# Graph-transformer layer: preparation of the edge loop by groups of x, and the rows of its first four steps gathered ahead

## What is computed

```python
xn = _layernorm(x, axis=-1)
...
x_l = (x @ W_l.T + b_l).reshape(n, HEADS, DIMS)
x_r = (x @ W_r.T + b_r).reshape(n, HEADS, DIMS)
...
s = x_l[src] + x_r[dst] + e_feat
s = jax.nn.leaky_relu(s, NEG_SLOPE)
alpha = jnp.einsum('ehc,hc->eh', s, att)
...
out = jax.ops.segment_sum(alpha[..., None] * x_l[src], dst, num_segments=n)
return out.reshape(n, FEAT) + bias
```

## Time and profile before

| | us |
|---|---|
| median of three runs | 3488.56 (3485.78 to 3489.42) |
| the profiled execution | 3486.59 |
| its span, first to last instruction | 3484.9 |
| preparation, to the edge loop's first instruction | 138.59 |
| edge loop's steps | from there to about 1410 |
| rest: own part, mixer, experts | about 1410 to the end |

### The profile page before, as it was taken

The page is one execution under the profiler, slowest core; times in us unless marked ns, Lnnn a source line. Parts: engine busy times, 40 slices in busy tenths (PEclk is TensorE's granted clock), DMA queues, the critical chain, the costliest instruction groups (busy, mean ns, idle before and its releaser), DMA issues. The chain is left out here.

```text
span 3484.9 us, 52064 instructions
## 1 busy us (share of the span) xinstructions
PE 3136.0 (90%) x14323; PEld 2542.8 (73%) x14324; DVE 1877.1 (54%) x3779; ACT 1357.1 (39%) x4647; POOL 1244.5 (36%) x1197
## 2 busy tenths in 40 slices
PE   2799999999999999557998899889989986999988
PEld 1577777777777777346777677767767775888877
DVE  5577877777777877865436343643454340111002
ACT  0047767767777766431223122222312211222232
POOL 2276666666666664113103010300020016000016
PEclk9899999999999999678999999999989978999999
DMA  5576776677676676251101011000000043333333
GB/s 135 155 190 167 168 167 167 164 165 166 166 166 164 166 167 131 78 183 30 30 14 34 23 34 36 8 1 14 27 37 1 1 128 104 113 123 123 115 113 107
DMA packets 301651, 355.64 MB, mean 102 GB/s; under 512 B 164806, under 2 KB 223771, under 8 KB 297545
## 3 DMA queue, kind: packets, MB, share of 16 engines
q0 software_dynamic: 67472, 178.15, 20.1%
q1 hardware_dynamic: 233510, 173.64, 18.8%
q10 hardware_dynamic: 560, 2.35, 0.2%
HBM read 298.03 MB, written 54.91 MB: 101 GB/s over the span
## 5 line engine op out<-in xcount | busy, mean ns | idle before, releaser
L1311 PE MATMUL a_pS<-g_xr,a_lt 128*128 x1680 | 522.2, 393 | 28.0 <-DMA XS<-xl_d,a_ix 22.9
L1294 POOL DMA_INDIRECT a_g<-xl_d,a_ix x480 | 461.4, 961 | 222.4 <-PE a_pS L1312 135.0
L1405 ACT ACTIVATE b_m<-a_g,c_pcx 128x64 f32<-128x64 f32 x1856 | 454.6, 333 | 0.0
L1319 PE MATMUL b_pM<-b_m,b_oh 128*112 128x281 f32 x1680 | 445.3, 404 | 5.3 <-DVE g_acc L1447 3.5
L1440 DVE SCALAR_TENSOR_TENSOR a_r<-a_pS,g_attx 128x528 f32<-128x528 f32 x420 | 296.6, 706 | 243.8 <-PE a_pS L1312 234.8
L1294 POOL DMA_INDIRECT XS<-xl_d,a_ix x360 | 345.2, 959 | 135.3 <-issue 91.5
L113 POOL TENSOR_TENSOR m_rstd<-m_ve,m_mhalf 125x5 f32<-125x5 f32 x45 | 53.1, 1180 | 928.4 <-DVE m_ve L103 919.9
L1311 PEld LDWEIGHTS a_pS<-g_xr,a_lt 128*128 128x128 f32 x1680 | 310.0, 191 | 90.2 <-issue 33.3
L1319 PEld LDWEIGHTS b_pM<-b_m,b_oh 128*112 128x112 f32 x1680 | 292.1, 177 | 102.1 <-issue 11.4
L421 PE MATMUL m_pH<-m_h,m_w 128*128 128x312 f32 (+1 forms) x1280 | 341.9, 428 | 7.7 <-DVE m_h L566 7.7
L1405 ACT ACTIVATE b_m<-XS,c_pcx 128x64 f32<-128x64 f32 x1424 | 348.5, 333 | 0.0
(11 more groups left out here) (371 smaller groups left out, 4410.0 us busy)
## 6 DMA issues: line engine op xcount, KB each, us to landing
a_db<-dl_d SPq DMA_DIRECT2D x212, 224.0 KB
f_w<-in_ffn_W1p SPq DMA_DIRECT2D x32, 1024.0 KB
m_w<-in_mix_W SPq DMA_DIRECT2D x8, 1024.0 KB
f_w<-in_ffn_W2p SPq DMA_DIRECT2D x8, 1024.0 KB
a_g<-xl_d,a_ix POOLq DMA_INDIRECT x480, 5.7
xg_d<-m_zero POOLq DMA_DIRECT2D x1, 7168.0 KB, 30.5
a_lt<-eat_d SPq DMA_DIRECT2D x214, 32.0 KB, 4.1
eat_d<-a_stage SPq DMA_DIRECT2D x15, 448.0 KB
```

The source lines that it names most:

```text
L1294: p.indirect_dma_start(out=gathered(t)[:, j, :], out_offset=None, in_=xl_d, in_offset=bass.IndirectOffsetOnAxis(ap=IX[:, t // BSTEPS, n:n ...
L1311: pe.matmul(o, lt[:, j, :], XRW[:, bass.ds(ws[h], 1), :].rearrange("p a d -> p (a d)"), start=True, stop=False)
L1319: ins = pe.matmul(pM[0:WN, h, 0:MW], OH[:, b, j, :], M[:, b, j, :], start=(j == 2 * h), stop=(j == 2 * h + 1))
L1405: ins = a.activation(m[:, j, part], gathered(ts)[:, j, part], ACT.Copy, scale=of[:, first + j, h, 0:1])
```

## The change

Preparation:

- x comes by groups on two queues: groups 0, 2, 4 from SP, 1 and 3 from ACT, with `wlr`, `blr`, `bias` and `attx` on ACT as well.
- Each group goes its own way: statistics, root on POOL, normalise, turn, copy, the x_l windows that it completes (`READY` = 0, 5, 11, 16, 22, 28). All of x_l comes ahead of all of x_r. `pP` holds four single windows.
- ACT copies the turned groups and x_l, and stores each normalised group itself. The bias of x_l is no longer added: it goes into `bias` and into `blr[1]`.
- The item count stands behind the first group's normalisation and the weights' linear column. Its two tables are turned by one PE instruction (`pair`, `turned`) and stored as rows of 128 words.
- SP's stores of x_l come ahead of those of the edge tables. `ends` needs no cast, `ok` takes one instruction less, and the break tables stand at windows 16 to 21 in place of 20 to 25. ACT copies `DLX`.
- POOL, when all of `xn_d` and `xl_d` is stored, gathers the rows of steps 0 to 3 (`EARLY`) into `zone`, 16 gathers, and waits for them.

Edge loop: in the first round steps 0 to 3 gather nothing and wait for no rows; the first target and attribute loads go out ahead of the list of sources; `ACC` is cleared in seven pieces at steps 2 to 6, 9 and 10.

```diff
@@ sync, preparation
+                x_group(0)
                 sp.dma_start(ends_i[:, 0, :], ...)
                 sp.dma_start(ends_i[:, 1, :], ...)
...
+                x_group(2)
+                x_group(4)
...
+                xl_part(0)
+                xl_part(1)
+                sp.wait_ge(s["i_turned"], 1)
+                sp.dma_start(wl_d.rearrange("(c p) -> c p", p=128), turned[0:CH, :]).then_inc(s["i_wl"], 16)
...
@@ scalar, preparation
+                for q in range(NG):
+                    a.wait_ge(s["p_t_full"], q + 1)
+                    for k in range(KC):
+                        ins = a.activation(XT[:, k, ...], pT[:, GT * k:GT * k + GT, 0:P], ACT.Copy)
+                    ins.then_inc(s["p_t_out"], 1)
+                    a.wait_ge(s["p_ln_out"], GT * q + GT)
+                    a.dma_start(xn_d[:, q * GT:(q + 1) * GT, :], XS[:, q * GT:(q + 1) * GT, :]).then_inc(s["p_xn_d"], 16)
+                    for w in range(READY[q], READY[q + 1]):
+                        a.wait_ge(s["p_lr"], w + 1)
+                        a.activation(XL[:, w, :], pP[0:WN, w % 4, 0:GD], ACT.Copy).then_inc(s["p_xl"], 1)
@@ gpsimd, preparation
+                p.wait_ge(s["i_x_out"], 1)
+                p.wait_ge(s["p_t_full"], NG)
+                p.wait_ge(s["p_xn_d"], 16 * NG)
+                p.wait_ge(s["p_xl_d"], 16 * (NW // XW))
+                for n in range(IG * EARLY):
+                    p.indirect_dma_start(out=zone[:, n * GD:(n + 1) * GD], out_offset=None, in_=xl_d,
+                                         in_offset=bass.IndirectOffsetOnAxis(ap=SRCX[:, n:n + 1], axis=0)).then_inc(s["g_early"], 16)
+                p.wait_ge(s["g_early"], 16 * IG * EARLY)
@@ edge loop
+                        if at_start(i) and t < EARLY:
+                            return
...
+                        if at_start(i) and t in CLEARED:
+                            at_w = CLEAR_W * CLEARED.index(t)
+                            v.memset(ACC[:, at_w:at_w + CLEAR_W, :], 0.0).then_inc(s["b_zeroed"], 1)
-                    v.memset(ACC[:, :, :], 0.0).then_inc(s["b_zeroed"], 1)
```

More of the change, by code:

```diff
@@ L816, in graph_attention @@
             ends_i = sb("i_ends_i", [NW, 2, NTE], I32)
-            ends = sb("i_ends", [NW, 2, NTE])
-            below = ends
+            below = sb("i_below", [NW, 2, NTE])
             wbase = sb("i_wbase", [NW, 2])
@@ L849, in graph_attention @@
             anyT = sb("i_any_turned", [2 * CH, 128])
-            XW, TURNS = 4, 8
-            FLAGS = 20
+            XW = 4
+            READY = [0] + [(q + 1) * GN // WN for q in range(NG - 1)] + [NW]
+            TURNS, FLAGS, ANY_TURN = 4, 16, 24
             pN = c.enter_context(nc.psum_tensor("i_pN", [128, 512], F32))
@@ L979, in _ @@
-                pe.wait_ge(s["i_any"], 2)
-                pe.transpose(pN[0:2 * CH, 0:128], anyb[:, :, :].rearrange("p n c -> p (n c)"), ident[:, :]).then_inc(s["i_any_turned"], 1)
+                    if q == 0:
+                        pe.wait_ge(s["p_linear"], 1)
+                    elif q == NG - 1:
+                        pe.wait_ge(s["p_const"], 2)
+                    pe.wait_ge(s["p_t_out"], q + 1)
+                    for w in range(READY[q], READY[q + 1]):
+                        if w >= 4:
+                            pe.wait_ge(s["p_xl"], w - 3)
+                        window(0, w)
@@ new lines, in _ @@
+                index_turned(0)
+                for w in range(NW):
+                    if w < 4:
+                        pe.wait_ge(s["p_xl"], NW - 4 + w + 1)
+                    else:
+                        pe.wait_ge(s["p_xr"], w - 3)
+                    window(1, w)
+                    if 1 <= w - TURNS < 2 * CH:
+                        index_turned(w - TURNS)
+                    if w == ANY_TURN:
+                        pe.wait_ge(s["i_any"], 2)
+                        pe.transpose(pN[0:2 * CH, 0:128], anyb[:, :, :].rearrange("p n c -> p (n c)"), ident[:, :]).then_inc(s["i_any_turned"], 1)
@@ new lines, in _ @@
+                v.wait_ge(s["p_b_lr"], 16)
+                then(linear(blr[:, :, :].rearrange("p m (h d) -> p m h d", h=GH), 2, WN))
+                v.wait_ge(s["p_attx"], 32)
+                by_heads = bias[:, :].rearrange("p (h d) -> p h d", h=GH)
+                v.tensor_tensor(by_heads, by_heads, by_head(blr[:, 0, :])[:, :, 0:HD], ALU.add)
+                then(v.tensor_tensor(blr[:, 1, :], blr[:, 1, :], blr[:, 0, :], ALU.add))
+                half = by_head(attx[:, :])
+                v.tensor_scalar(half[:, :, 0:HD], half[:, :, 0:HD], 1.0 - SLOPE, None, ALU.mult)
@@ L1189, in exists, with at_start, rows_landed @@
                     return not isinstance(base, int) or 0 <= base + t + k < STEPS
+                def at_start(i):
+                    return isinstance(i, int) and i == 0
+                def rows_landed(i, t):
+                    return 64 * i if t < EARLY else 64 * i + 64
                 def chain_of(i, t):
```

280 lines of the change are left out of this document (149 added, 131 removed).

## The result

| | before | changed |
|---|---|---|
| median | 3487.59 us (4 runs) | 3447.75 us (4 runs, 3444.87 to 3452.45) |
| profiled execution | 3486.59 us | 3447.26 us, span 3445.4 |
| ratio | 1 | 0.9887, 95% interval 0.987 to 0.9904 |

A forecast was written before the change was run, and what follows sets the result against it. TensorE was taken to bound the running edge loop: 3486.59 less 34.6 (preparation) and 15.0 (loop's start) gives 3437.0, and with the runs' median 2.0 above the profiled execution, 3439 us; range 3424 to 3460.

The forecast's parts named there:

- rival 1: Preparation: five DMA engines become the bound, block ends at 112 to 118 us, total 3447 to 3453; chance 0.2.
- rival 2: Loop's start: early rows bring little, PE waits at the fifth step, gain 5 to 9 us, total 3445 to 3449; chance 0.12.
- rival 1's sign: Preparation: DVE waiting for the keys or for x past 5 us.
- x_l: Preparation: first window at 24.5 us, then windows, turns, copies and item tables take 42.3, ending at 67 us.
- x's landing: Preparation's start: x groups 0 and 1 share five DMA engines at 134 GB/s, both landed at 14 us.
- The fit: Loading x: 2.0 us plus bytes over 436 GB/s, both groups at 7.6 us; quoted but not adopted.
- The key: Preparation: key ready at about 76 us, store 6 to 8 and loads 5, back at 88 to 90.
- Gathering ahead: Preparation: 16 gathers start at 72 to 75 us, last lands at 95 to 98, hidden before 104.
- The block: Preparation ends at 104 us against 138.6, -34.6; bounds 96 and 118.
- The loop's start: Edge loop: first product 4.7 us in, twelfth step at 55.5 against 70.5, -15; bounds 5 and 20.
- Rival 4: Preparation: ScalarE held at its x_n stores, 16.37 us at each of five, stopping PE 82 us: 3521; chance 0.03.

The follow-up runs named there:

- e9: Changed kernel with every x load and x_n store issued as two transfers, partitions 0 to 111 and 112 to 124: 3616.45 us, kernel before 3676.45.
- e5: Changed kernel with x groups 0 and 1 both on SyncE's queue, group 3 moved up on ScalarE's, group 1's statistics later: 3626.26 us, kernel before 3668.72.
- e2: Changed kernel with ScalarE's two edge attribute stores issued only once the keys are back, after the destination table copies: 3629.55 us, kernel before 3674.49.
- e12: The kernel of e10 timed in five rounds beside the kernel before: 3436.44 us against 3485.94, ratio 0.9856.
- e11: Kernel before with only the clearing in seven pieces and the new order of first loads: 3669.76 us, kernel before 3676.45.
- e1: Changed kernel with the DRAM key row starting at element 128, so the key store's rows are aligned to 512 bytes: 3622.53 us, kernel before 3674.49.
- e3: Changed kernel with no rows gathered ahead (EARLY = 0): 3647.03 us, kernel before 3674.49.
- e8: e7 with the two attribute gathers put ahead of destination rows 1 to 6: 3623.37 us, kernel before 3668.72.
- e4: Kernel before with only the early gathers and the skipped gathers of steps 0 to 3 added: 3682.85 us, kernel before 3674.49.
- e6: Changed kernel with keys worked out before the x_r windows and stored ahead of the last two x_l parts: 3630.87 us, kernel before 3668.72.
- e7: e6 with three steps' rows gathered ahead, attribute stores behind x_l's, flags two windows later: 3627.80 us, kernel before 3668.72.
- e10: e7 and e9 together, against the kernel before: 3604.89 us, kernel before 3676.45.

## Why the prediction was right, and where it was not

*The mechanism was right, the sizes only in part.* TensorE bounds the loop, and what is saved ahead of it stays saved. But the forecast gave itself 100 to 108 for the preparation and -12 to -17 for the loop's start; 109.7 and -11.7 lie just outside both. The total, 3447.75, is one that rival 1 (3447 to 3453) and rival 2 (3445 to 3449) had priced, and rival 1's sign, VectorE waiting over 5 us for the keys, came with 12.3. What held is the range of 3424 to 3460, which had been drawn wide enough for these rivals.

*x_l.* Its time line was right to a microsecond at its end (67 forecast, 66.1 found), which is luck, for errors cancel in it: group 0 landed at 16.6 instead of 14 and the first five windows took 6.6 us instead of 4.4, while the four later turns cost 1.2 to 1.3 each instead of 2.3. ScalarE's copy cost 0.69 (0.77 put), the first window came 2.3 us late.

*x's landing.* "Whichever queue issues it" was right, and five engines too (0.31 of 16; e9). The term itself was mis-sized: 14 us was worked out as if groups 0 and 1 had these engines to themselves. In the first 10 us W_lr and the broadcasts pass as well (share 1.01 from 6 to 10 us). An estimate: they are 1.3 MB, five sixteenths of it are 0.4 MB, and at the 134 GB/s of five engines that is 3 us, where 2.6 are missing. It is the likely reason, but was not tried by itself, and e5 neither shows nor refutes it. And I took the five engines as a given, where they are a property of how the transfer is cut. The fit that the prediction quotes (2.0 us plus bytes over 436 GB/s) stands in the Trainium skill, "DMA: Bandwidth & Descriptors", section "Anatomy of one DMA — SWDGE (gpsimd) path", for transfers that GpSimd issues; these came from SyncE and ScalarE, and the trace has 16.6 where the fit gave 7.6.

*The key.* Forecast 6 to 8 for the store and 5 for the loads, found 14.9 and 7. The step that failed is the sentence "With x_n on the other queue I take 6 to 8": it blamed the queue, where it is the traffic beside the store. Without the attribute stores beside it the store took 7.2 (e2), with x and x_n cut over 16 engines 7.7 (e9). Rival 1 had this in words (x_n's last groups, x_l, the attributes "and the keys now meet between 55 and 95 us") and priced it at a block end of 112 to 118; 109.7 lies between the forecast and the rival.

*Gathering ahead.* "67 + 5 to 8 = 72 to 75" was the other mis-sized term: 82.5. With x and x_n cut over 16 engines it was 69.2 (e9). It alone puts the block's end at 108.5 to 109.7. I had called these gathers hidden by six microseconds; they were hidden by one at the most, and only because the keys were late as well.

*The block* ended 5.7 us after the forecast of 104.

*The loop's start.* First product + 4.3 (4.7 put), twelfth step + 58.9 (55.5 put): -11.7 instead of -15. Two things made it late. The first step took 6.3 us instead of 5.1, with a granted clock of 0.50 up to 117 us and 0.59 from 117 to 120, and the fifth began at + 22.8 instead of + 20.6. And GpSimd's first gather in the loop came at + 13.4 instead of + 11.5, so that "POOL's 5.0 us a step and PE's 3.6 to 5.2 run level" failed once: its gathers are back to back from there, some at 1.1 to 2.1 us instead of 0.95, and TensorE waited 3.3 us at the sixth step. Behind that wait the granted clock was 0.50 from 141 to 143 us, and the step took 5.3 us instead of 3.6. The forecast named the fifth as the place for rival 2; the mechanism is that rival's, rows that land 7 us after their issue, at a third to a half of its size. In e12 one step's lead less went with 2.6 to 3.6 us, though that kernel differs in more. The pieces of the clearing cost 0.99 each (0.95 put); that the old clearing stood in nobody's way fits e11 without being shown by it.

*Rival 4*, ScalarE held at its x_n stores, did not come in the changed kernel: they cost 0.26 to 0.28 each. In e12 two of them, now pairs, took 1.37 and 1.96 us. In e1 to e9 something held its copy of the last x group 1.9 to 3.5 us; what, is open.

## What to carry to other kernels

Before moving work past a loaded stretch, find the next bound behind each one that you remove: here two chains, keys and early rows, ended within about a microsecond of each other, and both hung on the same DMA engines; mending the keys alone gave nothing (e2), leaving the early rows out 1 to 3 us in the block, and more was lost in the loop (e3). Check also what your edit moves besides: in e5 and in e8 another transfer took the place of the one that was moved, and hid the effect that was looked for. When a stretch shows a DMA share of a third at the full pace of x, look at how the transfer is cut before you reorder anything: 125 partitions went over five engines, 112 and 13 over all. A gather ahead of a loop is worth its issue time for as long as the loop follows the gathering engine, and costs the block's end as soon as what it reads is late (e4).

## What the runs showed that was not expected

- A preparation block that its early gathers end is over 4.6 to 5.8 us after the end of the last one's issue (e2, e4, e6, e7, e8, e10 and e12): this tail belongs to the price of gathering ahead.
- Splitting 125 partitions into 112 and 13 took the DMA share of the x stretch from 0.33 to 1.03 and the rate from 132 to 269 GB/s. The busy engines tripled and the rate only doubled, so each of them moved less; why is open.
- A store of 0.46 MB, at the same place in the queue's order and of the same shape, took 7.2 us (e2), 7.7 (e9), 10.5 (e5), 11.0 (e3), 14.0 (e1) and 14.9 us by what ran beside it; 4 bytes of offset are the difference between the last two.
- In e6 the granted clock was 0.73 on average from 60 to 66 us and 0.77 from 66 to 74, that is 1.2 GHz for part of each, after TensorE had stood 4 us for a copy; the six windows behind it took 8.5 us instead of 5.6.
- The same kernel stood 71.6 us under the run of before beside it in e10, single runs, and 49.5 in e12, medians of four and seven. Why is open; a gain read from a single pair of runs is not to be carried over.
